# Adding the skip in the Toeplitz tile and copying the channels by matmul in the long convolution of a decoder kernel

## The reference, cut to what matters

```
kv = jnp.einsum('bhil,bhjl->bijhl', k_, v_)            # k_ = v_ = ctx, H = 32 heads of 8 channels, L = 512
y = irfft(rfft(kv, n=1024) * rfft(ssm_kernel, n=1024))[..., :L]    # a causal convolution over l
out = y + kv * D[None, None, None, :, None]            # the skip
out = jnp.einsum('bijhl,bhil->bjhl', out, q_)          # q_ = x
x = _layernorm(x + out)
```

## Time and profile before

| | |
|---|---|
| runs | 2414.85, 2418.88, 2418.99 us |
| the profiled execution | 2414.85 us, of it the span of the profile 2413.1 us |
| fifth stage in the trace | first DMA issue at 1812.0 us, last work at about 2050.4 us |
| its start, until the first matmul on `e_kv` | 1812.0 to 1847.5 us |
| its loop over heads | 1847.5 to 2022 us |
| its end | 2022 to 2050.4 us |
| busy over the whole span | PE 1857.4 us (77%), DVE 1519.6 (63%), ACT 908.7 (38%), POOL 475.4 (20%) |

### The profile page before, as it was taken

One profiled execution on the slowest core, in us unless ns is written; L12 is line 12 of the kernel. 1 busy time (PEld: TensorE's weight loads), 2 busy tenths in 40 slices (PEclk: granted clock), 3 DMA queues, 4 the chain that ended last, 5 costly groups with the idle time before them and its releaser, 6 DMA issues. The chain is left out here.

```text
span 2413.1 us, 33560 instructions
## 1 busy us (share of the span) xinstructions
PE 1857.4 (77%) x12432; PEld 1423.7 (59%) x12432; DVE 1519.6 (63%) x2879; ACT 908.7 (38%) x1557; POOL 475.4 (20%) x477
## 2 busy tenths in 40 slices
PE   3248888713376899999999977999976996178885
PEld 2225555412253799999999966787754775034443
DVE  8847677387476466666666654656662777357876
ACT  1015555500032444444444423222214112577784
POOL 0033232000001001010001001010101887024442
PEclk9859999856688999999999988999997998589897
DMA  4099999222364122222222213010004114601000
GB/s 192 0 148 142 150 150 150 51 91 70 128 217 152 41 59 75 65 62 74 74 62 63 68 57 108 19 36 18 19 14 173 48 50 148 239 0 36 26 22 22
DMA packets 149820, 200.05 MB, mean 83 GB/s; under 512 B 13408, under 2 KB 92128, under 8 KB 147232
## 3 DMA queue, kind: packets, MB, share of 16 engines
q1 hardware_dynamic: 138400, 176.99, 29.2%
q10 hardware_dynamic: 11264, 20.98, 2.3%
HBM read 151.43 MB, written 46.22 MB: 82 GB/s over the span
## 5 line engine op out<-in xcount | busy, mean ns | idle before, releaser
L453 DVE TENSOR_REDUCE a_rowmax<-a_ring 128x2 f32<-128x512 f32 x256 | 165.2, 688 | 101.3 <-PE a_ring L532 99.1
L1464 DVE TENSOR_TENSOR f_hid<-f_gate,f_gu 128x256 f32<-128x256 f32 x264 | 108.5, 421 | 163.5 <-ACT f_gate L1336 160.9
L1336 ACT ACTIVATE f_gate<-f_gu 128x256 f32<-128x256 f32 x264 | 98.3, 381 | 275.5 <-PE f_gu L1202 187.5
L2193 PE MATMUL e_py<-e_kv,e_toep 128*128 128x320 f32 x640 | 174.2, 436 | 2.9 <-DVE e_kv L2217 2.9
L405 ACT ACTIVATE a_prob<-a_sT 128x1024 f32<-128x1024 f32 x128 | 130.6, 1026 | 82.5 <-PE a_sT L521 82.2
L2193 PEld LDWEIGHTS e_py<-e_kv,e_toep 128*128 128x128 f32 x640 | 122.7, 192 | 54.2 <-issue 4.4
L1215 PE MATMUL f_gu<-f_lowh,f_bg 128*128 128x256 f32 x704 | 141.3, 283 | 5.2 <-POOL f_lowl L1121 5.0
L1202 PE MATMUL f_gu<-f_xhi,f_wg 128*128 128x256 f32 x704 | 130.3, 283 | 0.0
L1202 PE MATMUL f_gu<-f_xhi,f_wu 128*128 128x256 f32 x704 | 129.2, 282 | 0.0
L1215 PEld LDWEIGHTS f_gu<-f_lowh,f_bg 128*128 128x128 f32 x704 | 115.7, 191 | 9.7 <-POOL f_lowl L1121 5.2
L1469 DVE TENSOR_TENSOR f_hl<-f_hid,f_hh 128x768 fp32r<-128x768 f32 (+2 forms) x90 | 84.5, 939 | 55.9 <-ACT f_hh L1382 54.8
(11 more groups left out here) (363 smaller groups left out, 4925.0 us busy)
## 6 DMA issues: line engine op xcount, KB each, us to landing
f_entry<-in_WdT SPq DMA_DIRECT2D x89, 256.0 KB, 2.8
a_qs<-parts SPq DMA_DIRECT2D x96, 128.0 KB, 6.3
a_ks<-parts SPq DMA_DIRECT2D x96, 128.0 KB, 7.1
parts<-a_hi SPq DMA_DIRECT2D x16, 512.0 KB, 9.0
parts<-a_lo SPq DMA_DIRECT2D x16, 512.0 KB, 9.3
e_toep<-lags SPq DMA_DIRECT2D x32, 256.0 KB
f_entry<-in_Bg SPq DMA_DIRECT2D x89, 64.0 KB, 1.8
f_entry<-in_Bu SPq DMA_DIRECT2D x89, 64.0 KB, 2.0
```

The costliest lines, as they stand in the source:

```text
L453: dve.tensor_reduce(rowmax[:, s % 2, :, e * SLOTS + j], ring[n % RING][:, :].rearrange("p (q t) -> p q t", t=T), AX.X, ALU.max, negate=Tru ...
L1336: act.activation(gate[:, i % 2, :], gu[n % 3][:, 0, :], ACT.Silu).then_inc(s_["gate_ready"], 1)
L1464: dve.tensor_tensor(hid[:, j, :], gate[:, i % 2, :], gu[n % 3][:, 1, :], ALU.mult).then_inc(s_["hid_ready"], 1)
L2193: last = pe.matmul(py[n % RING][:, 0:DIAG * BS], toep[:, h % 3, (t - j) * P:(t - j + 1) * P], kv[:, h % 2, :, j, :], start=(j == 0), stop= ...
```

## The change

- The scratch tensor `lags`, the tile `e_lags` and POOL's addition go. The Toeplitz tiles are loaded straight from the input `taps`; the first three are issued after the first, second and third block of loads instead of after the second, third and fourth. SyncE no longer waits for the addition and for the write.
- The skip is added in the loaded tile: POOL makes a constant 128 x 128 matrix `swap` with ones on the anti-diagonal, and DVE computes swap * skip[h] + toep on the first 128 columns, once per head (`toep_ready`). DVE now waits for the Toeplitz load, PE for `toep_ready`.
- `put` moves from ACT to PE: four matmuls of 64 columns with the identity as weights. put(0) stands before the wait for x, and put(h+1) ahead of the ten matmuls of head h.
- `e_kv` is laid out by tile of l first, so that the 320 columns of a matmul are one run of memory, and the products are made in four instructions of 320 columns, each announced by itself.

The core of the diff:

```diff
@@ sync
-                    row = io["lags"][h:h + 1, :]
+                    row = io["taps"][h:h + 1, :]
...
-                sp.dma_start(lags[:, :], io["taps"]).then_inc(s_["got_taps"], 16)
-                sp.dma_start(skip[:, :], io["skip"].rearrange("o h -> h o")).then_inc(s_["got_taps"], 16)
+                sp.dma_start(skip[:, :], io["skip"].broadcast_to([P, SH])).then_inc(s_["got_skip"], 16)
...
-                    if k == 0:
-                        sp.wait_ge(s_["skip_added"], 1)
-                        sp.dma_start(io["lags"], lags[:, :]).then_inc(s_["taps_out"], 16)
-                    else:
-                        sp.wait_ge(s_["taps_out"], 16)
-                        taps(k - 1)
+                    if k < 3:
+                        taps(k)
...
-                sp.wait_ge(s_["kv_ready"], SH)
+                sp.wait_ge(s_["kv_ready"], SH * KT)
@@ gpsimd
-                pool.tensor_tensor(lags[:, P:P + 1], lags[:, P:P + 1], skip[:, :], ALU.add).then_inc(s_["skip_added"], 1)
+                pool.memset(swap[:, :], 0.0).then_inc(s_["swap_made"], 1)
+                pool.wait_ge(s_["swap_made"], 1)
+                pool.affine_select(out=swap[:, :], in_=swap[:, :], compare_op=ALU.not_equal, fill=1.0,
+                                   base=-(P - 1), pattern=[[1, P]], channel_multiplier=1).then_inc(s_["swap_made"], 1)
@@ scalar
-                def put(h):
-                    if h >= 2:
-                        act.wait_ge(s_["kv_ready"], h - 1)
...
-                    act.activation(pt[h % 2][:, 0:KT * BS].rearrange("p (n i) -> p n i", i=SD), every(h, 0, 1)[:, 0, :, :],
-                                   ACT.Copy).then_inc(s_["c_ready"], 1)
-                put(0)
-                put(1)
                 for h in range(SH):
-                    if h + 2 < SH:
-                        put(h + 2)
@@ tensor
+                def put(h):
+                    if h == 0:
+                        pe.wait_ge(s_["c_copied"], 2 * KT)
+                    if h >= 2:
+                        pe.wait_ge(s_["kv_ready"], (h - 1) * KT)
+                    for t in range(KT):
+                        last = pe.matmul(pt[h % 2][:, t * BS:(t + 1) * BS], keep["ident"][:, :], cx[:, t, :, h, 0:SD],
+                                         start=True, stop=True)
+                    last.then_inc(s_["c_ready"], 1)
...
+                put(0)
                 pe.wait_ge(s_["q_ready"], 2 * NT)
                 for h in range(SH):
-                    pe.wait_ge(got_t[h % 3], 16 * (h // 3 + 1))
-                    pe.wait_ge(s_["kv_ready"], h + 1)
+                    if h + 1 < SH:
+                        put(h + 1)
+                    pe.wait_ge(s_["toep_ready"], h + 1)
                     for t in range(KT):
                         n = h * KT + t
+                        pe.wait_ge(s_["kv_ready"], n + 1)
...
-                                             kv[:, h % 2, :, j, :], start=(j == 0), stop=(j == t))
+                                             kv[:, h % 2, j, :], start=(j == 0), stop=(j == t))
@@ vector, products(h)
+                    dve.wait_ge(got_t[h % 3], 16 * (h // 3 + 1))
+                    dve.scalar_tensor_tensor(toep[:, h % 3, 0:P], swap[:, :], skip[:, h:h + 1], toep[:, h % 3, 0:P],
+                                             ALU.mult, ALU.add).then_inc(s_["toep_ready"], 1)
                     dve.wait_ge(s_["c_ready"], h + 1)
                     if h >= 2:
                         dve.wait_ge(s_["y_done"], (h - 1) * KT)
-                    c = pt[u][:, 0:KT * BS].rearrange("p (n i) -> p n i", i=SD)
-                    dve.tensor_tensor(kv[:, u, :, :, :].rearrange("p d t (b i) -> p d (t b) i", i=SD),
-                                      c.unsqueeze(1).broadcast_to([P, DIAG, KT * B, SD]), every(h, 0, DIAG), ALU.mult
-                                      ).then_inc(s_["kv_ready"], 1)
+                    for t in range(KT):
+                        c = pt[u][:, t * BS:(t + 1) * BS].rearrange("p (b i) -> p b i", i=SD)
+                        dve.tensor_tensor(pairs(kv[:, u, t, :]), c.unsqueeze(1).broadcast_to([P, DIAG, B, SD]),
+                                          shifted(t, cx, h, DIAG), ALU.mult).then_inc(s_["kv_ready"], 1)
```

More of the change, by code:

```diff
@@ L728 @@
 SCRATCH = {"parts": ([2, 2, 2, D // 2, T], F32), "ctxT": ([D, N], F32)}
-SCRATCH |= {"lags": ([SH, P + D], F32)}
 SCRATCH |= {f"x{n}": ([N, D], F32) for n in range(1, 6)}
@@ L2027, in long_convolution @@
         zf = mk.sb("e_zf", [P, KT, N])
-        skip = mk.sb("e_skip", [SH, 1])
-        lags = mk.sb("e_lags", [SH, P + D])
+        skip = mk.sb("e_skip", [P, SH])
+        swap = mk.sb("e_swap", [P, P])
         xt = mk.sb("e_xt", [P, 4, D])
         toep = mk.sb("e_toep", [P, 3, D])
-        kv = mk.sb("e_kv", [P, 2, DIAG, KT, BS])
+        kv = mk.sb("e_kv", [P, 2, KT, DIAG * BS])
         planes = mk.sb("e_planes", [P, 2, KT, SD, B, WIDE])
@@ L2037, in long_convolution @@
         resid = cx[:, :, :, :, :].rearrange("p k b s i -> p (k b s i)")
-        names = ("got_taps", "skip_added", "taps_out", "x_turned", "q_ready", "c_ready", "c_copied", "kv_ready", "y_done",
+        names = ("got_skip", "swap_made", "x_turned", "q_ready", "c_ready", "c_copied", "toep_ready", "kv_ready", "y_done",
                  "z_ready", "z_wrapped", "z_added", "add_steps", "z_turned", "added", "mean_ready", "square_ready",
@@ L2046, in long_convolution @@
         stored = sem("e_stored")
-        def every(h, first, diagonals):
-            at = cx[:, 0, :, h, first:]
-            return bass.AP(tensor=at.tensor, offset=at.offset, ap=[at.ap[0], [1, diagonals], [SH * WIDE, KT * B], [1, SD]])
         def shifted(t, wide, h, diagonals):
@@ L2107, in _ @@
             def _(pool):
-                pool.wait_ge(s_["got_taps"], 32)
-                pool.tensor_tensor(lags[:, P:P + 1], lags[:, P:P + 1], skip[:, :], ALU.add).then_inc(s_["skip_added"], 1)
+                pool.memset(swap[:, :], 0.0).then_inc(s_["swap_made"], 1)
+                pool.wait_ge(s_["swap_made"], 1)
+                pool.affine_select(out=swap[:, :], in_=swap[:, :], compare_op=ALU.not_equal, fill=1.0,
+                                   base=-(P - 1), pattern=[[1, P]], channel_multiplier=1).then_inc(s_["swap_made"], 1)
                 ch = Chain(pool, s_["add_steps"])
@@ L2141, in _ @@
                                        ).then_inc(s_["q_ready"], 1)
-                def put(h):
-                    if h >= 2:
-                        act.wait_ge(s_["kv_ready"], h - 1)
-                    else:
-                        act.wait_ge(s_["c_copied"], 2 * KT)
-                    act.activation(pt[h % 2][:, 0:KT * BS].rearrange("p (n i) -> p n i", i=SD), every(h, 0, 1)[:, 0, :, :],
-                                   ACT.Copy).then_inc(s_["c_ready"], 1)
-                put(0)
-                put(1)
                 for h in range(SH):
-                    if h + 2 < SH:
-                        put(h + 2)
                     act.wait_ge(s_["z_ready"], (h + 1) * KT)
@@ L2215, in products @@
                         dve.wait_ge(s_["y_done"], (h - 1) * KT)
-                    c = pt[u][:, 0:KT * BS].rearrange("p (n i) -> p n i", i=SD)
-                    dve.tensor_tensor(kv[:, u, :, :, :].rearrange("p d t (b i) -> p d (t b) i", i=SD),
-                                      c.unsqueeze(1).broadcast_to([P, DIAG, KT * B, SD]), every(h, 0, DIAG), ALU.mult
-                                      ).then_inc(s_["kv_ready"], 1)
+                    for t in range(KT):
+                        c = pt[u][:, t * BS:(t + 1) * BS].rearrange("p (b i) -> p b i", i=SD)
+                        dve.tensor_tensor(pairs(kv[:, u, t, :]), c.unsqueeze(1).broadcast_to([P, DIAG, B, SD]),
+                                          shifted(t, cx, h, DIAG), ALU.mult).then_inc(s_["kv_ready"], 1)
+                dve.wait_ge(s_["got_skip"], 16)
+                dve.wait_ge(s_["swap_made"], 2)
                 products(0)
```

## The result

The changed kernel is slower. The median of four runs is 2448.72 us (2445.05 to 2452.39) against 2418.93 us (2414.85 to 2421.34) of four runs before, a ratio of 1.0128 with an interval of 1.0111 to 1.0144. Three more executions of the changed kernel, not in that median, took 2443.69, 2449.22 and 2451.96 us. The forecast was 2445.0 us in a range of 2433 to 2454. The profiled execution took 2443.69 us with a span of 2441.9; before it was 2414.85 with 2413.1, so the two profiles lie 28.8 us apart.

The account below looks back on a forecast made before the run. PE was taken to bound the fifth stage's loop at 5.38 us a head; +27.3 us for put and -1.2 for the start gave +26.1, 2445.0 us on the median 2418.88, range 2433 to 2454.

Parts of the forecast that it names:

- PE is the bound of the loop: Fifth stage's loop: PE busy 174.2 of 174.5 us, without a hole; an instruction added to it is paid in full.
- put, 0.88 us a head: PE in the loop: four 64-column matmuls make 8 records of 0.110 us a head, 27.3 us for 31.
- A load behind a long record is not paid: PE in the loop: put's first weight load hides under the last long record, so 8 loads a head are paid.
- 31 heads: Loop of the fifth stage: 31 of 32 puts lie in it, put(0) ahead; 248 records, 27.3 us.
- The start, -1.2 us: Before the loop: loads net 0, PE no longer idles before the first head; between -2.9 and +0.6, middle taken.
- DVE's extra work, 0.50 us a head, hidden: DVE in the loop: products in four +0.21 us, skip 0.29 at most; fits under PE's period, cost 0.
- Waits on PE: PE's added waits for kv, toep_ready and put's PSUM tile: signalled early, cost 0, at most 1.6 us.
- Layout of kv: PE's matmul reads in the loop: one run of 320 rather than 5 of 64; a gain is not possible.
- 1 (columns alone, 0.43 us a head): put on PE: load hides or is saved, a record costs its columns; 13.3 us, 2431 us total; chance 0.07.
- 2 (load plus columns): put on PE: load and columns add up, or runs of 8 cost as much; 39.9 to 42.4 us; chance 0.05.
- 3, no change: Loop: the head period stays near 5.4 us and the time does not change; chance 0.03.
- 4: DVE in the loop: a late Toeplitz load makes DVE the bound, 43 us above the sum; chance 0.03.

## Why the prediction was right, and where its terms were off

- *PE is the bound of the loop; what is added to it is paid in full.* Right. put alone on the kernel before brings the new period of 6.28 us, and put back on ACT restores 5.38.
- *put, 0.88 us a head.* Measured 0.90, by 0.1125 us a record. The reason given is that a short record costs the load behind it. The widths show that it is not the columns: four matmuls of 64 and of 96 columns cost the same, and two of 128 half as much. That the fixed cost is the load is an inference, from its 0.11 us and from the loads of other widths. The prediction took it from records at half clock, 0.107 us when scaled to full. The trace of before has short fp32 records at a granted clock of 1.00 too, four of 8 columns at line 1164: their loads take 0.52 us from 789.36 on, the last of them 0.19, so they start 0.11 us apart. The upper value, 0.117 us, is the distance of the records of 256 columns in the earlier trace rows, (1501.38 - 1500.33)/9. That distance is not shown to bound the load of a short fp32 record. The 0.110 us was the author's choice between the two; the runs show 0.1125.
- *A load behind a long record is not paid.* The trace of before shows it in two ways. In the loop PE is busy for 174.19 of 174.53 us and its weight loads for 122.67 of the same time, so the loads run beside the matmuls. And from 320 columns (0.2692 us) to 512 (0.4275 us) a record grows by 0.82 ns a column, so 320 columns alone would take 0.264 us, an estimate from the earlier trace rows. That leaves 0.005 us a record, where a load paid in full would need 0.107.
- *31 heads.* This was a mistake in the count: 30 puts stand between the first long matmul and the last. put(1) comes ahead of head 0's matmuls, and the prediction counted it a second time in the start. Right is 30 x 0.90 = 27.0 us, where it had 27.3.
- *The start, -1.2 us.* The profile has -1.33 until the first long matmul and 1.8 - 1.1 = 0.7 us less lost to the clock in the first head, -2.0 together. The parts came out otherwise than worked out: the loads, taken as 0, gave 1.7 us in the first profile; put ran at half clock, and from the last transposes' start to the first long matmul it took 0.4 us more. With a higher clock, as in the second profile of the changed kernel, PE waits 0.66 us for ACT's last copies of q before put(1): a limit that the prediction did not name, since it let both puts run through. That -1.2 lay near was luck: it was the middle of a range of 3.5 us.
- *DVE's extra work, 0.50 us a head, hidden.* It is 0.46 us, and hidden even under the old period. *Waits on PE:* nothing, as taken: with one wait a head the period stays 6.28 us. The 0.05 us a head that the prediction allows them at most is shown by no run. *Layout of kv:* the sum has nothing for it, and nothing came: the long records keep their distance, and a head's 20 take 5.38 us with put on ACT.
- *The Toeplitz load lands in time.* The trace shows no wait of DVE for it in the loop.
- The sum: 27.0 - 2.0 = 25.0 us, and the stage grew by 24.9; forecast 26.1. The forecast is 1.1 us too high: the head too many makes +0.9, the start +0.8, and the price of put -0.6. The measured medians were 29.8 us apart the first time (26.9 to 34.8 by the interval) and 23.7 the second (19.9 to 27.1). The other kernels with this period lay 25.8 (96 columns), 26.5 (one wait), 27.1 (put alone) and 27.9 us (put spread) above the kernel before. The 24.9 us lie below the first interval, so some 2 us or more of that comparison are not explained by the stage. The profiles show that other stages differ between executions by as much, but not why.
- The rivals: 1 (columns alone, 0.43 us a head) is refuted by the period with 64 columns, though it is the price once four matmuls are made one. 2 (load plus columns) is refuted by the 96 columns. Its price of 0.161 to 0.171 us a record is not met either: these runs show 0.1125. 3, no change, did not occur: put on PE cost 0.43 us a head in its cheapest form. 4 did not occur: in the loop PE waited for no engine.

## What to carry to other kernels

Read first which engine has no hole in the loop. Work moved from an idle engine to that one was paid in full here, though it was small (0.90 us a head); work added on an engine with idle time was free (0.46 us out of 1.24 us of waiting). When a copy on TensorE can't be avoided, make it of few and wide matmuls: from 64 to 128 columns an fp32 matmul cost the same 0.225 us, and spreading the short ones between long ones hid nothing more.

## What the runs showed of the hardware that was not expected

- An fp32 matmul of 64 or 96 columns costs 2 x 0.1125 us, of 128 columns the same, of 256 columns 2 x 0.215. The same identity four times in a row saves no load: the trace has 256 loads for put's 256 records, and the price stays.
- A short fp32 matmul between two long ones hides nothing more than eight short records in a row: the period is 6.27 us against 6.28. Its two records fit that, if only the first one's load lies under a long record.
- The same program ran put at the start once at a granted clock of 0.50 (16 records in 3.3 us) and once at 0.88 (8 in 1.14 us). The first head then took 6.57 us at 0.83 and 5.44 at 1.00, and in the run with one wait a head 8.03 us at 0.68.
- With the context's loads on a second queue the first transpose of x came 3 us later (10.5 against 7.4 us after the first issue) and the first long matmul 2.6 us later (35.6 against 33.0).
